# Six batch tiles instead of five: the first 512 rows of a feature-interaction tower cut into 128, 128 and 256 rows, all in array tiles of 64 rows by 32 columns

## The reference

```
e = stack([tbl_f[ids[:, f]] for f in range(32)], axis=1)        # 2048 x 32 x 64
z = concatenate([sum(e, axis=-1),
                 einsum('bpd,pde,bpe->bp', e[:, II, :], kernels, e[:, JJ, :])], axis=1)
h = concatenate([z, dense_ctx], axis=1)                         # 544 columns
h = maximum(h @ W_top1 + b_top1, 0)                             # 512
h = maximum(h @ W_top2 + b_top2, 0)                             # 256
y = h @ W_top3                                                  # 2048 x 1
```

## Time and profile before

| | |
|---|---|
| three runs | 843.25, 843.35, 846.5 us |
| the profiled execution | 841.05 us |
| its span, first to last instruction | 839.2 us |
| granted TensorE clock over the span | 1.000 |
| TensorE matmul busy | 804.7 us (96%) |
| VectorE busy | 616.2 us (73%) |
| ScalarE busy | 142.4 us (17%) |
| GpSimd busy | 484.0 us (58%), 512 gathers |

### The profile page before, as it was taken

How to read it: one execution, slowest core, us unless ns; L and a number is a source line. 1 busy time by engine, 2 the same in 40 slices (tenths; PEclk the granted TensorE clock), 3 DMA queues, 4 the chain that set the end, 5 groups by cost and what they waited for, 6 DMA issues and landing times.

```text
span 839.2 us, 33255 instructions
## 1 busy us (share of the span) xinstructions
PE 804.7 (96%) x15452; PEld 367.9 (44%) x15452; DVE 616.2 (73%) x613; ACT 142.4 (17%) x219; POOL 484.0 (58%) x518
## 2 busy tenths in 40 slices
PE   0699999999999999999999999999999999999998
PEld 0267767677754433333333333333333333333333
DVE  0477886588867788889855678988854588988850
ACT  0211022212120320120210320021111212011002
POOL 6777777777777777777777567767743340000000
PEclk9999999999999999999999999999999999999999
DMA  9611111111111111111111111111100010000000
GB/s 327 211 31 31 31 31 30 29 32 34 30 29 28 29 29 29 31 29 29 29 27 27 22 26 28 29 28 28 29 17 14 14 20 2 2 2 2 2 3 0
DMA packets 24387, 29.44 MB, mean 35 GB/s; under 512 B 13365, under 2 KB 13623, under 8 KB 24122
## 3 DMA queue, kind: packets, MB, share of 16 engines
q0 software_dynamic: 16384, 16.81, 10.2%
q1 hardware_dynamic: 7856, 10.49, 3.7%
q10 hardware_dynamic: 10, 0.01, 0.0%
HBM read 27.27 MB, written 0.01 MB: 33 GB/s over the span
## 4 chain that ended last, share of the span: by engine, by line
PE 93%; POOL 2%; DVE 2%; issue 1%; DMA 1%; ACT 0%; DVEq 0%; ACTq 0%
PE y L618 52%; PE accs L636 25%; PE y L598 4%; PE y L680 4%; PE y L668 3%; PE y L697 3%; POOL rows L371 2%; DVE prod L563 2%; PE y L673 1%; PE y L710 1%; DMA rows<-tbl,ids_sb 1%; PE y L649 0%; DMA ids_sb<-ids 0%; DVEq L265 0%; ACT h L484 0%
## 5 line engine op out<-in xcount | busy, mean ns | idle before, releaser
L563 DVE TENSOR_TENSOR prod<-y,xt 128x1024 f32<-128x1024 f32 (+1 forms) x525 | 576.4, 1157 | 170.9 <-PE y L618 167.5
L371 POOL DMA_INDIRECT rows<-tbl,ids_sb x512 | 483.3, 944 | 201.8 <-issue 125.1
L618 PE MATMUL y<-xt,kw 64*32 64x512 f32 (+1 forms) x9920 | 471.2, 509 | 5.6 <-DVE prod L563 2.2
L618 PEld LDWEIGHTS y<-xt,kw 64*32 64x32 f32 x9920 | 185.6, 107 | 245.3 <-issue 218.6
L636 PE MATMUL accs<-prod,ones_strip 64*32 64x512 f32 (+1 forms) x4960 | 242.6, 504 | 1.1 <-issue 0.6
L636 PEld LDWEIGHTS accs<-prod,ones_strip 64*32 64x32 f32 x4960 | 106.4, 107 | 110.3 <-issue 102.6
L417 ACT COPY xt<-y 128x1024 f32<-128x1024 f32 (+2 forms) x48 | 34.9, 728 | 381.8 <-PE y L598 381.8
L598 PE MATMUL y<-ident,rows 128*128 128x128 f32 x256 | 39.7, 289 | 24.8 <-DMA rows<-tbl,ids_sb 24.8
L535 DVE TENSOR_REDUCE z_rows<-rows 128x8 f32<-128x512 f32 (+1 forms) x80 | 42.9, 568 | 20.8 <-DMA rows<-tbl,ids_sb 20.8
L598 PEld LDWEIGHTS y<-ident,rows 128*128 128x128 f32 x256 | 27.6, 143 | 53.9 <-issue 39.6
L448 ACT COPY h_in<-accs 128x1024 f32<-128x1024 f32 (+1 forms) x10 | 8.4, 841 | 144.0 <-PE accs L636 144.0
(11 more groups left out here) (22 smaller groups left out, 61.9 us busy)
## 6 DMA issues: line engine op xcount, KB each, us to landing
rows<-tbl,ids_sb POOLq DMA_INDIRECT x512
kw<-pair_k SPq DMA_DIRECT2D x14, 512.0 KB, 10.2
w_sb<-w SPq DMA_DIRECT2D x1, 1024.0 KB
w_sb<-w SPq DMA_DIRECT2D x1, 512.0 KB
kw<-pair_k SPq DMA_DIRECT2D x1, 384.0 KB, 16.5
kw<-pair_k SPq DMA_DIRECT2D x1, 256.0 KB, 3.8
w1z_sb<-w1z SPq DMA_DIRECT2D x1, 256.0 KB
ids_sb<-ids SPq DMA_DIRECT2D x1, 224.0 KB, 2.6
```

Source lines behind the costliest of these rows:

```text
L371: pool.indirect_dma_start(out=rows[:, s, c, h, :], out_offset=None, in_=tables[f], in_offset=bass.IndirectOffsetOnAxis(ap=ids_sb[:, b, f:f ...
L563: nc.vector.tensor_tensor(prod_part(t, d, n), y_part(t, d, n), x, ALU.mult).then_inc(y_read, n)
L618: last = nc.tensor.matmul(y[columns, h, :], kw[part, d, columns], xt[part, slot_of(t, units[h][0] // 2), 0:w], start=True, stop=True)
```

## The change

Three values change, and everything that hangs on them: the batch tiles are 128, 128, 256, 512, 512 and 512 rows wide, and `SPLIT_WIDTH` goes to 128, so that the steps of the 128-row batch tiles are also issued with 32 columns of weights at a time (line 83).

```diff
-WIDTHS = [256, 256, 512, 512, 512]
+WIDTHS = [128, 128, 256, 512, 512, 512]
-SPLIT_WIDTH = 256
+SPLIT_WIDTH = 128
```

## The result

The changed kernel takes 915.9 us (median of four runs, 914.74 to 916.62) against 843.45 for the kernel before: a ratio of 1.0851, 95% interval 1.0828 to 1.0874. The forecast was 846, its range ended at 857. The profiled execution took 916.0 us, with a span of 914.1 and a mean granted clock of 0.991.

A forecast was written before the change was run, and what follows sets the result against it. GpSimd's gathers were taken to bound the short batch tiles, allowing at most 3.0 us. The start's -4.9 us is absorbed, GpSimd's pause nets +2.5 on 841.05 profiled: 843.5, median 846 us; range 840 to 857.

The forecast's parts named there:

- The bound by the gathers: GpSimd's gathers follow without a pause, so TensorE can be at most 3.0 us earlier after the short batch tiles.
- step 116: In the last short batch tile, where TensorE transposes the next tile's couples: 227.22 us before, forecast 229.75.
- gather 176: Last gather for couples 4 and 5 of the first 512-row batch tile; landed by 224.25 us before, forecast 229.75.
- Pace of a round: Eight matmul instructions, one on each array tile, take 0.112 us at 128 columns, from a line through two widths.
- the burst at 23.48: Timeline stretch with 8 matmuls and 16 weight loads under way in 0.1 us, taken as showing that issue keeps up.
- Part 1: Start of batch tile 0: step 0 at 18.6 us instead of 23.49, a gain of 4.9.
- Parts 2 and 3: Steps 0 to 39, then 40 to 111 of tile 0: step 40 at 38 us, GpSimd pauses 5.5, 2.5 us later.
- Gather 49: First gather for couple 8 of batch tile 1; waits for a slot until 68.5 us instead of starting at 62.95.
- rival 4: Part 3's mechanism with larger sizes: GpSimd pauses 8 to 12 us, +5 to +9, 850 us; 15%.
- Part 4: Rest of TensorE's own way through the short batch tiles: step 116 at 221.4 us, 8.3 before the gathers.
- Rival 3: Instruction blocks of 256 come each 2.3 us, 0.144 us a round: +14 us, 857 us; 12%.
- Rival 2: 128-column rounds take about 0.2 us, nearly as long as 256-column ones: +49 us, 892 us; 12%.

The follow-up runs named there:

- e16: Kernel before, with sum groups of 2 banks instead of 4 in its two 256-row batch tiles; 835.36 us, ratio 0.9898.
- e1: Changed kernel with SPLIT_WIDTH back at 256, so steps of the 128-row batch tiles use 128 columns of weights; 856.38 us, ratio 1.0136 to the kernel before.
- e2: Kernel before, with each 512-column step matmul of the last batch tile issued as four of 128 columns; 945.55 us (before 844.57).
- e3: Kernel before, with each 512-column step matmul of the last batch tile issued as two of 256 columns; 845.38 us (before 844.57).
- e7: e2, but with 128 columns of weights in the last batch tile's steps, so as few instructions as before; 859.26 us (before 841.78).
- e11: e1 with sum groups of 2 banks instead of 4 in the two 128-row batch tiles; 845.45 us, ratio 1.0012 to the kernel before.
- e13: e11 with 12 instead of 8 slots for gathered couples; 844.56 us, ratio 1.0022 to the kernel before.
- e10: Kernel before with SPLIT_WIDTH 512 and the middle 512-row batch tile cut into 256 and 256; 866.12 us, ratio 1.0243.
- e17: Kernel before with SPLIT_WIDTH 512 and sum groups of 2 banks in its two 256-row batch tiles; 848.2 us, ratio 1.0059.
- e14: Changed kernel with sum groups of 2 banks instead of 4 in the 128-row batch tiles; 908.22 us (one run).

## Why the prediction was wrong

**The bound by the gathers (right in place, too tight in size).** In e16 TensorE comes to step 116 at 221.00 and is held until 223.93 by gather 176, and from there on the kernels with the same late tiles take nearly the same time: 612.0 us to the end before, 610.9 in the changed kernel, 611.4 in e1, 610.3 in e16. But e16's span is 5.0 us shorter and its median 8.9. The 3.0 us were read off one execution of 841.05 us, where the median is 843.35. Up to step 116, e2, e3 and e7 run the code of the kernel before, and they come there at 228.27, 229.81 and 231.35, not at 227.22; so the room was 3 to 7 us.

**Pace of a round (right inside a block, wrong as a rate).** 0.112 us was forecast and 0.112 measured, over 63 matmuls. The failed step is that I took the burst at 23.48 and a line through two widths for a sustained pace. Sustained, a round takes 3.9 / 16 = 0.244 us, since its 16 instructions come no faster, and that makes up 59 of the 76 us (61.2 against 2.5 us of gaps after a packet, in the table under e16). At 256 columns the array takes 128 x 0.2175 / 8 = 3.5 us for 256 instructions, already less than the 3.9 in which they come; in the kernel before, transposes, MLP parts and waits for VectorE let the supply nearly keep up (2.3 to 5.4 us of such gaps in four executions of its code). The line was drawn through a point next to the limit.

**Part 1, the start (right).** Step 0 came at 17.69 against 18.6 (17.54 + 1.15 is 18.7).

**Parts 2 and 3 (right without the supply limit).** Couple 10 at step 40 was to come at 38: 38.13 in e1, 45.94 in the changed kernel. Gather 49 was forecast at 68.5 and came at 71.78 in e11; its step 116 at 232.7 against 229.75; its time 845.45 against 846. The mechanism, GpSimd's pause for a slot, is there, but the pause is 8.8 us (71.78 against 62.96 for gather 49 before), as in rival 4, not 5.5, and TensorE's own way is only 1.2 us ahead of the gathers, not 8.3. So the near agreement of 845.45 with 846 is partly luck.

**Part 4 (too low, and its cover gone).** TensorE alone was to be at step 116 at 221.4; without pauses it is there at 231.5 (e13), and with the supply limit at 303.25. The third tile's fixed cost was under-priced; e10 has it at 20 us where it is bare, 14 without its slower wide weights. The sign of being wrong that the prediction named, TensorE at step 116 after 235 with no gather waited for, is what came.

**The rivals.** Rival 3 named the mechanism and had 12%. Its price was the mis-sized term: 2.3 us for a block of 256 instructions, where 3.9 was measured. The sum behind it was wrong too: a transfer of 1.09 us and a gather's 1.6 before its first data are 2.7, not 2.3. And it priced the wrong thing. From a packet's start to TensorE going on it takes 2.0 to 2.6 us (e2), much as priced, but the next packet starts only 0.8 to 2.0 us later, and the period is both. With 3.9 us a round is 16 / 256 of it, 0.244 us, and by the rival's own formula TensorE comes to step 116 at 221.4 + 624 x 0.132 = 303.8; measured 303.25. That agreement is partly luck, as 221.4 was 10 us low and the last term too high by about as much. Rival 2's cause, rounds that are slow on the array, is excluded: 63 matmul instructions in a row start 14 ns apart.

By the Trainium skill (Runtime: NRT & Kernel Launch, "Instruction fetch mechanics") instructions come in blocks of 256, the next fetched while one executes, hidden because issue is slower. The trace agrees with the blocks and with a packet that starts while one is executed, and not with the hiding: 256 are issued in about 2 us, and the next are there after 3.9. The floor of 25 ns that the Trainium skill gives (TensorE: Matmul & The Clock Gate, "Wait — 56ns, not 53.3ns?") doesn't hold between different array tiles: 0.88 / 63 is 14 ns.

## What to carry to other kernels

Count TensorE's instructions for each microsecond, not only columns: with float32 in eight array tiles a step is 32 instructions, and on this chip 256 of them need 3.9 us, so work cut so narrowly that the array would use them up sooner runs at the pace of the fetch. The sign in a profile is idle TensorE with "issue" as its releaser, in the middle of a loop without waits, at equal counts of matmuls. A stretch near the limit pays a few us already (2.3 to 5.4 in the kernel before). Smaller groups of sums gained 1.0% there (e16), more than any narrower tile, and by its trace mostly by sparing TensorE waits for VectorE. A bound read off one execution carries the spread between executions (227.22 to 231.35 us at one point here). A pace read at one width is a rate only up to the next limit: ask which resource goes with the number of instructions, and how near it is.

## What the runs showed of the hardware that was not expected

- TensorE's instructions come in blocks of 256, each about 3.9 us after the last when it waits for them (four in 15.74 us in the changed kernel; 16.65 us for four in e2, after the last gather, one of them mostly filled with sums of 512 columns). The packet itself takes about 914.1 x 16 x 0.011 / 146 = 1.1 us. TensorE goes on about 1.4 us after it has ended, and the next packet starts 0.8 to 2.0 us after that (e2). Why it does not start earlier, no row shows.
- Within a block, 63 matmuls with their weight loads on different array tiles took 0.88 us: 7 ns an instruction.
- A change between 64 by 128 and 64 by 32 array tiles and back costs an estimated 0.18 us, from e17 against e10.
- With gaps of about 2 us the granted clock is at the half level (1.2 GHz) in places: 0.94 on average from 40 to 120 us in the changed kernel, 0.98 in e14 and 1.00 in e1. It should cost little here, by an estimate: 16 rounds of 0.21 us, the half pace of the first steps, still fit into 3.9 us. No run tests it.
